# A decoder layer on one Trainium2 core: gathered expert tiles in 39 places of their own instead of a ring of 8

## The reference

```python
x = _layernorm(x + _L0_attn_ref(x, ...))                 # a chunked state-space mixer
x = _layernorm(x + _L0_xattn_ref(x, ctx_1024, ...))      # cross attention, 16 heads of 8
x = _layernorm(x + _L0_ffn_ref(x, gate_kernel, w0, w1, wo))
```

```python
weights, selected_experts = jax.lax.top_k(gate_logits, TOPK)        # TOPK = 2 of E = 8
weights = jax.nn.softmax(weights.astype(jnp.float32), axis=-1)
...
layer_1 = _gmm(sorted_hidden, w0, onehot)       # rows sorted by expert, 128 -> 512
layer_2 = _gmm(sorted_hidden, w1, onehot)
intermediate = jax.nn.silu(layer_1) * layer_2
layer_3 = _gmm(intermediate, wo, onehot)        # 512 -> 128
out = sum over the two choices of weights * layer_3 at the token's row
```

## Time and profile before

| | us |
|---|---|
| median of 3 runs | 509.08 |
| lowest, highest | 508.83, 510.47 |
| the profiled execution | 508.15 |
| its span | 506.8 |
| busy in the span: PE, DVE, ACT, POOL | 377.8, 304.8, 227.5, 244.4 |
| up to the first gather, start of line 1571 | 338.05 |
| first to last scatter, starts of line 1578 | 355.14 to 483.83 |

### The profile page before, as it was taken

One profiled execution on the slowest core, in us unless ns is written; L12 is line 12 of the kernel. 1 busy time (PEld: TensorE's weight loads), 2 busy tenths in 40 slices (PEclk: granted clock), 3 DMA queues, 4 the chain that ended last, 5 costly groups with the idle time before them and its releaser, 6 DMA issues.

```text
span 506.8 us, 7843 instructions
## 1 busy us (share of the span) xinstructions
PE 377.8 (75%) x2473; PEld 254.6 (50%) x2473; DVE 304.8 (60%) x778; ACT 227.5 (45%) x455; POOL 244.4 (48%) x309
## 2 busy tenths in 40 slices
PE   3997687877898788787576968218997898888900
PEld 1765555554444465443233424116886687676800
DVE  2655346786768878888987374413545455364635
ACT  2775544124656654646373732013534354353504
POOL 3723676443333415135566665534564555553316
PEclk9997557555759886957675555557899899998975
DMA  8731316355040404161232310011111111111052
GB/s 289 279 107 63 95 52 174 87 137 156 25 136 4 126 4 126 35 179 57 63 118 63 119 42 13 12 53 36 33 43 32 40 39 38 41 32 33 22 181 84
DMA packets 40312, 41.42 MB, mean 82 GB/s; under 512 B 5041, under 2 KB 34033, under 8 KB 40273
## 3 DMA queue, kind: packets, MB, share of 16 engines
q1 hardware_dynamic: 35888, 34.06, 22.2%
q0 software_dynamic: 3520, 5.25, 3.9%
q10 hardware_dynamic: 864, 1.61, 0.9%
HBM read 26.91 MB, written 13.73 MB: 80 GB/s over the span
## 4 chain that ended last, share of the span: by engine, by line
PE 48%; DVE 23%; issue 8%; POOL 6%; another core or an unknown queue 5%; ACT 5%; DMA 3%; DVEq 0%; ACTq 0%; POOLq 0%; SPq 0%
PE banks L886 9%; DVE nm L1079 7%; PE banks L794 4%; PE banks L746 4%; PE banks L909 4%; DVE topf L1141 3%; PE banks L694 3%; PE banks L617 3%; PE banks L714 2%; PE banks L898 2%; POOL table_dram L1553 2%; PE banks L737 1%; PE banks L910 1%; PE banks L704 1%
## 5 line engine op out<-in xcount | busy, mean ns | idle before, releaser
L1380 ACT ACTIVATE probs_all<-banks 128x1024 f32<-128x1024 f32 x64 | 65.5, 1023 | 67.7 <-PE banks L746 65.5
L1079 DVE TENSOR_REDUCE nm<-banks 128x4 f32<-128x1024 f32 x64 | 78.0, 1218 | 15.6 <-PE banks L737 14.5
L886 PE MATMUL banks<-w_split,scores_in 128*128 x234 | 68.5, 431 | 3.6 <-DVE scores_in L1223 2.8
L1578 POOL DMA_INDIRECT y_dram<-avT,scatter_u x39 | 38.2, 979 | 59.6 <-DVE avT L1229 53.5
L794 PE MATMUL banks<-probs_all,vals 128*9 128x256 f32 x512 | 55.2, 515 | 2.3 <-DVE avT L1095 1.2
L746 PE MATMUL banks<-scores_in 32*128 32x256 f32 x256 | 42.7, 420 | 16.6 <-DVE nm L1079 14.5
L1210 DVE TENSOR_TENSOR ctx_in<-ctx_in,banks 128x512 f32<-128x512 f32 x39 | 26.7, 684 | 41.1 <-issue 26.4
L886 PEld LDWEIGHTS banks<-w_split,scores_in 128*128 128x128 f32 x234 | 43.9, 203 | 13.5 <-issue 6.3
L909 PE MATMUL banks<-w_split,scores_in 128*128 x156 | 42.4, 349 | 8.1 <-DVE scores_in L1216 7.7
L737 PE MATMUL banks<-scores_in 32*128 32x256 f32 x256 | 42.4, 418 | 6.2 <-DVE nm L1079 6.0
L1571 POOL DMA_INDIRECT scores_in<-x_dram,gather_i x39 | 37.4, 959 | 18.0 <-issue 11.6
(11 more groups left out here) (212 smaller groups left out, 785.5 us busy)
## 6 DMA issues: line engine op xcount, KB each, us to landing
scores_in<-k_dram SPq DMA_DIRECT2D x32, 128.0 KB, 2.8
scores_in<-q_dram SPq DMA_DIRECT2D x32, 128.0 KB, 3.1
ctx_in<-in_L_ffn_w SPq DMA_DIRECT2D x16, 256.0 KB, 2.6
cs_wide<-cs_dram SPq DMA_DIRECT2D x14, 256.0 KB, 3.7
k_dram<-split_qk SPq DMA_DIRECT2D x8, 256.0 KB, 2.5
q_dram<-split_qk SPq DMA_DIRECT2D x8, 256.0 KB, 2.2
ctx_in<-in_L_ffn_wo SPq DMA_DIRECT2D x8, 256.0 KB, 2.8
x_in<-in_x SPq DMA_DIRECT2D x4, 256.0 KB, 5.2
```

Source lines behind the costliest of these rows:

```text
L886: m = TE.matmul(bank(2 * slot + j), xT[:, i % XT, xh, :], all_weights[:, c + j * FF:][:, bass.ds(expert_at[i], FF)], start=n == 0, stop=n ...
L1079: V.tensor_reduce(most, maxima_of(n).rearrange("p (j k q) -> p j k q", j=2, k=TPS), AX_X, ALU.max, negate=True).then_inc(s["nmax"], 1)
L1380: C.activation(probs(n).rearrange("p j k q -> p (j k q)"), EXPS, ACT.Exp, scale=SCALE).then_inc(s["probs"], 1)
L1578: G.indirect_dma_start(y_dram[:, :], bass.IndirectOffsetOnAxis(ap=scatter_u[:, i:i + 1], axis=0), y_slot[:, i % Y_RING, :], None).then_inc ...
```

## The change

Three things change. Every one of the 39 gathered tiles gets its own 128 columns of `xg`, so `xg` takes 4992 columns instead of 1024, and `xT` and `hsT` move up behind it (7808 of 8192 columns are then used). Since this region reaches into the queries, a gather now waits for the last exponent matmul of the attention (`exp_mm`) instead of for the transpose of eight tiles before. The gathers are issued sooner: twelve ahead of the first step, and then two with each step instead of one. And the eight arrival semaphores count groups of tiles with a growing size: tile 0; tile 1; tiles 2, 3; 4 to 6; 7 to 11; 12 to 18; 19 to 27; 28 to 38. A transpose waits until its whole group has landed.

```diff
-XG, AHEAD = 8, 6
+XG_GROUPS = (0, 1, 2, 4, 7, 12, 19, 28, SLOT_TILES)
+AHEAD, GATHERS = 12, 2
...
     for i in range(SLOT_TILES + 2):
-        if i + AHEAD < SLOT_TILES:
-            yield "gather", i + AHEAD
+        for g in range(AHEAD + GATHERS * i, min(AHEAD + GATHERS * (i + 1), SLOT_TILES)):
+            yield "gather", g
...
-        xg_end, xT_end = XG * D, (XG + 2 * XT) * D
-        xg = flat_q[:, 0:xg_end].bitcast(F32).rearrange("p (n d) -> p n d", n=XG)
+        xg_end, xT_end = SLOT_TILES * D, (SLOT_TILES + 2 * XT) * D
+        xg = flat_q[:, 0:xg_end].bitcast(F32).rearrange("p (n d) -> p n d", n=SLOT_TILES)
...
+        def gather_group(i):
+
+            g = sum(i >= n for n in XG_GROUPS) - 1
+            return g, XG_GROUPS[g + 1] - XG_GROUPS[g]
...
             def turn_x2(i):
-                q.wait_ge(a[f"g{i % XG}"], 16 * (i // XG + 1))
+                g, size = gather_group(i)
+                q.wait_ge(a[f"g{g}"], 16 * size)
...
-                TE.transpose(shared(i)[1], xg[:, i % XG, :], ident).then_inc(s["xg_t"], 1)
+                TE.transpose(shared(i)[1], xg[:, i, :], ident).then_inc(s["xg_t"], 1)
...
             def gather(i):
                 q.wait_ge(s["steps_v"], GATHER_ROWS)
-                q.wait_ge(s["xg_t"], i - XG + 1)
                 q.wait_ge(a["x2_out"], 16 * B)
+                q.wait_ge(s["exp_mm"], NPAIR)
                 G.indirect_dma_start(
-                    xg[:, i % XG, :], None, x2_dram[:, :],
-                    bass.IndirectOffsetOnAxis(ap=gather_i[:, i:i + 1].bitcast(U32), axis=0)).then_inc(a[f"g{i % XG}"], 16)
+                    xg[:, i, :], None, x2_dram[:, :],
+                    bass.IndirectOffsetOnAxis(ap=gather_i[:, i:i + 1].bitcast(U32), axis=0)).then_inc(a[f"g{gather_group(i)[0]}"], 16)
```

## The result

Timed beside the kernel before, the changed kernel took 517.01 us (median of 513.91, 514.31, 519.72 and 522.09) against 508.95 (median of 501.65, 508.83, 509.08 and 510.47). The medians' quotient is 1.0158; ratios in this document leave out runs in a slower state of the chip, and this one is 1.0229, 95% interval 1.0157 to 1.0301. So the change costs some 1 to 3%, and its size is not known better than that. The forecast was 504.7 us. The time is close to that of the rival that I called "slower", 516.4 us. The profiled execution took 513.91 us, its span is 512.6 (before 506.8).

The account below looks back on a forecast made before the run. PE was taken as nearly the bound, with holes from POOL's dense indirect DMAs. Profiled 508.15 us + 0.1 (wait) - 14.0 (saving) + 9.5 (cost) = 503.8, plus 0.9 for the median: 504.7 us; range 495 to 516, faster 0.48.

Parts of the forecast that it names:

- The reading of the bound: Expert stage: PE nearly the bound, with holes where POOL's dense indirect DMAs delay PE's completions; 25.7 us in nine ACT waits.
- Waits, places, groups: Gathers and transposes: the first gather's extra wait costs 0.1 us; dropped waits, moved buffers and waiting for whole groups cost 0.
- POOL's order: Eighteen gathers before the first scatter, at 360.7 us; last gather at 401.7 instead of 458.68; late scatters delay nobody.
- The scatters' lag: DVE's adds needing landed scatters: lag grows at most 1 us a step over ten steps, with 13 us spare; 0 us.
- The saving: Tiles 13 to 38, after the earlier last gather: holes go, 2.86 us a tile; 14.0 us saved, at most 17.4.
- The cost: Before tile 13: 21 more gathers at 0.45 us each delay PE; 9.5 us, bounds 0 to 21.3.
- The upper bound: Limit of the cost before tile 13: each of steps 3 to 13 takes 5.57 us instead of 3.63; 21.3 us.
- The slower rival: Up to tile 13, POOL's unbroken run of 50 DMAs makes every tile take 5.57 us; +7.3, 516.4 us; chance 0.30.
- No change: Expert stage: delays don't hang on POOL's DMAs, or saving and cost cancel; 509.1 us, within 0.3%; chance 0.22.

Follow-up runs that it names:

- Places alone: Changed kernel with own places kept, but POOL's order and semaphores of the kernel before: 506.85 us, ratio 1.0033 to the kernel before.
- the fifth chip: Both kernels rerun unchanged on a chip where the kernel before takes 480.98 us: changed kernel 482.83 us, ratio 1.0019; kernel before against itself 1.0074.
- the third: Changed kernel rerun as control on a chip where the kernel before takes 479.5 us: 486.78 us, ratio 1.0114.
- the chip of the first runs: Chip where the kernel before takes 504.61 us; four edits of the changed kernel ran there, not the changed kernel itself: 506.85, 518.56, 479.01 and 505.26 us.

## Why the prediction was wrong

**The reading of the bound: right where the delay exists.** POOL's dense DMAs make the holes: the gathers moved to SP took away all of them and 25 us. The recorded reading left out a third line of ACT with 3.5 us of such waits, which changes nothing in it. The 5% of the chain under "another core or an unknown queue" was worth its face value: 25 us of 506.8, and the page without holes lacks exactly that entry.

**Waits, places, groups: right.** Line 876, the transpose of a gathered tile, has to the digit what the earlier trace rows have:

```profile
  DMA scores_in<-x_dram,gather_i: 7.3, 4
```

Places alone: ratio 1.0033.

**POOL's order: right but for one issue, wrong about what waits.** The first scatter was to come 22.65 us after the first gather; on the fifth chip it comes after 358.85 - 336.29 = 22.56. On the chip of the result it comes after 28.15, because DVE was late (5.91 us of waiting), and the last gather is 77.7 us after the first, not 63.7. (The recorded sum counted one issue too many: the 50th DMA starts 31 issues of 1.28 us after the 19th, 62.4 us after the first; on the fifth chip it was 62.1.) The scatters' lag, set to 0 with 13 us in hand, isn't quite 0: 4.1 us of DVE's waits on the fifth chip, 1.1 us of PE (6.9 and 2.0 on the third). It was hidden on the chip of the result, where PE itself was late.

**The saving: right.** 14.0 us forecast, 15.3 measured, 2.86 us a tile after the last late completion at 416.29. Of the 3.4 us that I left for spells at half clock 1.3 were not needed.

**The cost: the step that failed.** 9.5 us forecast, at most 21.3; measured 24.15, beyond my own upper bound. The step took a price for each DMA, 0.45 us, out of a run of six, and multiplied. The traces fit a price that doesn't go by the DMA but by the run: once POOL has issued for some time without a pause, PE's completions stay back, and PE stops when its buffers are used up, until the run is over. A run of six would end before this bites in full. For the first run of eighteen instead of nine, tile 4 starts 29.6 us after the first gather instead of 19.8 (357.88 in the timeline of before): 9.8 us of the 24.15, or 1.1 for each of nine gathers where the step had 0.45. The other 14.4 come between tiles 4 and 13, where POOL issued a scatter and two gathers for each tile, in bursts of 9, 6, 3, 9 and 5; only 0.6 us lie between the 6 and the 3, and at the other ends it waits over 3 us for DVE or has issued the last gather (before, no burst after the first run had more than six). That run length is the cause is an inference from these traces: the edit that puts gaps into the run had no delay to act on. The upper bound failed for the same reason: it took 5.57 us, the longest interval that I had looked at, as the worst possible. The trace of before itself has 6.24 (tile 16 at 397.02 to tile 17 at 403.26), and the longest is now 364.63 - 352.96 = 11.67. The sum also had nothing for the clock that falls when PE waits, the 3.1 us estimated above.

**The slower rival** had the sign, the time and the deciding point (tile 13 later than 401.5; it was 408.64), but not the form: not every tile took 5.57 us; five took 6.5 to 11.7 and the others 2.85 to 4.9. That its total came so near is luck: in the traces its cost was 2.9 us too low and its saving 1.3, the stage began 3.0 us sooner, and the median lies 3.1 us above the profiled execution. I gave it 0.30 against 0.48. What spoke for it, that both runs of POOL I had looked at ended with a hole and PE went on when POOL paused, was the mechanism itself and deserved the larger share. The first nine gathers were in the profile, too: tiles 3 and 4 came 4.95 and 4.45 us after their predecessors there. I wrote that PE hardly ran then, and took no price from the longest run in the trace.

**No change** was a matter of the chip. Four of the five chips of the experiments show no delay in any trace; on the two of them where the changed kernel itself ran, POOL issues 60 DMAs in a row and PE isn't held back by them. The rule I weighed (the Trainium skill, "SBUF — State Buffer", section "Who interferes with whom"), that no DMA contends with a compute engine, agrees with these. On the chip of the first runs and on that of the result it doesn't: completions come up to 13.9 us late in the trace of the result, and the measurement decides. Nothing in one trace of before could tell that the kernel's 509 us would be 479 elsewhere.

What stays open: how POOL's DMAs reach PE's completions; whether PE sends them late or ACT sees them late, since in this stage no engine but ACT waits first for PE (ACT's own signals released DVE at once, 360.53 + 0.60 to 361.16); why on some chips and not others (or whether it is a state of a chip that passes, since no chip was met both with and without it), and whether fewer rows or gaps would help there.

## What to carry to other kernels

Before you price a DMA pattern per instruction, look whether what it delays is paid by the run: find the longest run in the trace, and see when the waiting engine goes on; if that is a fixed time after the run's end, the price of lengthening it is the whole of what is added, and no short run bounds it. A share of the chain with no owner can be time to be had, here 25 us, and it can belong to the chip: run the same kernel on another before you tune against it. Where the operation allows it, SP's queue is the safer place for a DMA beside dense TensorE work: about 479 us with the gathers on SP, on the chip with the delay and on the one without where it was tried. Those DMAs fetched rows in order, not the rows that the layer needs.

## What the hardware showed that I had not expected

- The same program takes 479 to 481 us on four chips, and 504.6 and 509 us in two sets of runs (whether these two were one chip isn't recorded), steadily within each set: 501 to 511 in 19 runs there, 477 to 486 in 31 on another chip. From tile 2 to tile 38 the stage takes 127.9 us in the trace of before and 102.9 in that of the fifth chip: 25.0 of the 29.1 us between the spans lie where the late completions are.
- POOL itself isn't slowed: full gathers issued back to back start 1.25 us apart, with the delay or without.
- PE goes on for a while when its completions are late: tile 3's up matmuls start at 352.96, while ACT learns of tile 2's, which ended at 346.60, at 360.53. So PE's timeline doesn't show where the delay begins; that of its consumer does.
